# A softplus sum moved from VectorE to TensorE with its string begun sooner, and three in place of two tiles of a shared product made by VectorE

## What is computed

```
x_dbl = xh @ W_x                       # 8 columns dt_low, 16 columns B, 16 columns C
dt = softplus(dt_low @ W_dt + b_dt)    # 256 inner channels
h  = exp(dt * A) * h + dt * B * xh     # 16 states per inner channel, one step per pixel
y  = sum_n(h * C) + xh * D
y  = y * silu(z);  out = y @ W_out
```

## Time and profile before

| | us |
|---|---|
| median of 3 runs | 13842.76 (13840.99 to 13844.69) |
| the profiled execution, its time | 13837.79 |
| its span | 13836.0 |
| DVE busy | 13466.6 (97%) |
| POOL busy | 13246.6 (96%) |
| ACT busy | 12104.2 (87%) |
| PE busy, matmul | 10079.9 (73%), granted clock 0.815 of full |

### The profile page before, as it was taken

The page is one execution under the profiler, slowest core; times in us unless marked ns, Lnnn a source line. Parts: engine busy times, 40 slices in busy tenths (PEclk is TensorE's granted clock), DMA queues, the critical chain, the costliest instruction groups (busy, mean ns, idle before and its releaser), DMA issues.

```text
span 13836.0 us, 170380 instructions
## 1 busy us (share of the span) xinstructions
PE 10079.9 (73%) x34752; PEld 2897.7 (21%) x34752; DVE 13466.6 (97%) x12084; ACT 12104.2 (87%) x24809; POOL 13246.6 (96%) x3076
## 2 busy tenths in 40 slices
PE   6777777777777777777777777777777777777776
PEld 1222222222222222222222222222222222222221
DVE  7999999999999999999999999999999999999999
ACT  7888888888888888888988888888898888888888
POOL 6999999999999999999999999999999999999999
PEclk8888888888888888888878888788888888888887
DMA  6667676666766676666667666666666666666665
GB/s 146 161 154 161 155 163 156 158 157 157 164 156 160 152 163 158 160 157 156 158 159 164 153 163 151 163 159 156 161 153 163 156 161 156 160 156 163 158 155 128
DMA packets 1195180, 2175.99 MB, mean 157 GB/s; under 512 B 152321, under 2 KB 161594, under 8 KB 1194042
## 3 DMA queue, kind: packets, MB, share of 16 engines
q1 hardware_dynamic: 1192762, 2164.07, 66.7%
q10 hardware_dynamic: 1280, 0.02, 0.0%
HBM read 1811.17 MB, written 352.32 MB: 156 GB/s over the span
## 4 chain that ended last, share of the span: by engine, by line
POOL 53%; issue 32%; DVE 6%; ACT 5%; PE 1%; DMA 1%; SPq 0%; POOLq 0%; ACTq 0%; DVEq 0%
POOL hq L1064 38%; POOL dbx L1054 15%; DVE hq L946 4%; ACT ps_a L640 2%; DVE dbx L929 1%; ACT dbx L654 1%; DMA b_rep<-bc_d 0%; DMA dt_d<-dt 0%; DVE pp L905 0%; ACT xh L600 0%; ACT L600 0%; ACT L765 0%; PE ps_acc L456 0%; DMA dtx_d<-sp 0%; POOLq L1063 0%
## 5 line engine op out<-in xcount | busy, mean ns | idle before, releaser
L1064 POOL TENSOR_TENSOR hq<-hq,c_rep 128x2048 f32<-128x2048 f32 x2048 | 9251.0, 4535 | 468.8 <-ACT carry L659 465.0
L946 DVE TENSOR_TENSOR_SCAN hq<-ps_a,dbx 128x512 f32<-128x512 f32 x8192 | 9443.6, 1207 | 128.8 <-ACT dbx L654 47.2
L640 ACT ACTIVATE ps_a<-dt_rep,A_neg 128x512 f32<-128x512 f32 x8192 | 5625.2, 687 | 1294.7 <-DVE hq L946 1231.5
L1054 POOL TENSOR_TENSOR dbx<-dtx_rep,b_rep 128x2048 f32<-128x2048 f32 (+1 forms) x1024 | 4082.1, 3986 | 99.1 <-DMA dtx_rep<-dtx_d 89.1
L654 ACT ACTIVATE dbx<-ps_a,dbx,carry 128x1 f32<-128x1 f32 x7168 | 2504.9, 349 | 240.2 <-POOL dbx L1054 140.4
L929 DVE TENSOR_TENSOR dbx<-dtx_rep,ps_b 128x2048 f32<-128x2048 f32 (+1 forms) x1280 | 2626.7, 2052 | 9.5 <-PE ps_b L444 9.3
L456 PE MATMUL ps_acc<-hq,dsum 128*32 128x512 f32 x16384 | 2334.0, 643 | 292.6 <-POOL hq L1064 292.6
L382 PE MATMUL pp<-sq,w_b1T 128*128 128x512 f32 x512 | 531.1, 1141 | 1608.7 <-ACT sq L579 1608.7
L444 PE MATMUL ps_b<-dbl,bsel 41*128 41x512 f32 x2560 | 1587.3, 703 | 153.3 <-DVE dbx L929 97.7
L400 PE MATMUL pp<-x,W_taps 128*128 128x512 f32 x768 | 693.3, 1002 | 895.2 <-DVE x L900 531.4
L456 PEld LDWEIGHTS ps_acc<-hq,dsum 128*32 128x32 f32 x16384 | 355.9, 111 | 1865.7 <-issue 1046.5
(11 more groups left out here) (123 smaller groups left out, 10466.4 us busy)
## 6 DMA issues: line engine op xcount, KB each, us to landing
dtx_rep<-dtx_d SPq DMA_DIRECT2D x2048, 256.0 KB, 5.4
dt_rep<-dt_d SPq DMA_DIRECT2D x2048, 256.0 KB, 6.3
c_rep<-bc_d SPq DMA_DIRECT2D x1024, 256.0 KB, 4.7
xr<-in_x SPq DMA_DIRECT2D x704, 256.0 KB, 10.9
b_rep<-bc_d SPq DMA_DIRECT2D x2048, 64.0 KB, 5.5
dtx_d<-sp SPq DMA_DIRECT2D x256, 512.0 KB, 2.8
dt_d<-dt SPq DMA_DIRECT2D x256, 512.0 KB, 6.1
xin<-in_x SPq DMA_DIRECT2D x256, 256.0 KB, 10.2
```

The source lines that it names most:

```text
L640: A(ps_a[:, BANK[i], :], dt_rep[:, q // NQ, g, :], ACT.Exp, scale=A_neg[:, q // NQ, q % NQ, g:g + 1]).then_inc(exp_done, 1)
L946: v.tensor_tensor_scan(hq[:, q % HQ, g, :], ps_a[:, BANK[i], :], dbx[:, slot(q), g, :], 0.0, ALU.mult, ALU.add).then_inc(scan_done, 1)
L1054: g.tensor_tensor(dbx[:, slot(q), m:, :], dtx_rep[:, d, m:, :], b_rep[:, q % NQ // 2, :].unsqueeze(1).to_broadcast([P, DG - m, T]), ALU.mu ...
L1064: g.tensor_tensor(quad, quad, c_rep[:, c % 2, q % NQ, :].unsqueeze(1).to_broadcast([P, DG, T]), ALU.mult).then_inc(cmul_done, 1)
```

## The change

VectorE's `softplus` (L905) is removed. W_dt is halved once at the start, so that TensorE leaves v/2 in PSUM. ACT takes |v/2| into `sp` (Abs), exp(-2 |v/2|) into `dt` and ln(1 + that) in place. TensorE adds `sp` and then `dt` onto v/2 in PSUM by matmuls with the identity (`step_sum`, two matmuls of 512 columns each time, in its slots 12 and 14): v/2 + |v/2| = max(v, 0). The last of them raises the semaphore that `dt_x` waits for. On ACT, `evac_dbl` moves from slot 9 to 8, the three steps of the string from 12, 13, 14 to 11, 12, 13, the pooling parts from 10, 11 to 14, 15. The wait for the DMA of the chunk before out of `dt` moves from `evac_dt` to the Exp. On PE, `step_dt` stays in slot 10 but stands ahead of `sum_states` there, and the convolution moves from 11, 12, 13 to 13, 15, 16. `SPLIT` becomes 3: of the shared group DVE makes three tiles, POOL one.

```diff
@@ -53,9 +53,10 @@
 NB = 2
 
 PE_XH, PE_Z, PE_DBL, PE_DT, PE_OUT = (1, 2), (3, 5), 7, 10, 20
-PE_CONV = (11, 12, 13)
+PE_STEP = (12, 14)
+PE_CONV = (13, 15, 16)
 PE_Y, PE_GC, PE_VAR = 19, 24, 27
-ACT_XZ, ACT_DBL, ACT_SP, ACT_DT, ACT_OUT = 5, 9, (12, 13, 14), 17, 23
+ACT_XZ, ACT_DBL, ACT_SP, ACT_DT, ACT_OUT = 5, 8, (11, 12, 13), 17, 23
 ACT_CONV, ACT_GELU, ACT_SQ, ACT_RSTD = 18, 21, 26, 29
 DVE_NORM, DVE_Y1, DVE_DT, DVE_Y0, DVE_GATE = 0, 8, 16, 24, 23
 GN_STATS, GN_SUM, GN_MOM, GN_RSTD, GN_SCALE, GN_SILU = 24, 25, 25, 27, 28, 29
@@ -76,10 +77,10 @@
 assert all(BANK[tile] == BANK[tile - AGE[tile]] for tile in range(NT))
 
 BY_DVE = (0, 2, 3, 4, 6)
-ND, SHARED, SPLIT = len(BY_DVE), 3, 2
+ND, SHARED, SPLIT = len(BY_DVE), 3, 3
 PE_SHARED, DVE_SHARED = 6, 8
 
-POOL_CHUNKS, POOL_SLOTS, ATT_CHUNK = (1, 2, 3, 4), (10, 11), CH - 4
+POOL_CHUNKS, POOL_SLOTS, ATT_CHUNK = (1, 2, 3, 4), (14, 15), CH - 4
 TAP_SPREAD, TAP_MM, TAP_KEEP, TAP_DIAG = 24, 26, 28, (30, 31)
 ATT_FC, ATT_H, ATT_MM, ATT_SUM, ATT_EXP, ATT_WTS = 24, 25, 26, 28, 29, 31
 
@@ -375,6 +376,13 @@
                 if kw == 2:
                     last.then_inc(conv_done, 1)
 
+            def step_sum(b, c, k):
+                pe.wait_ge(sp_done, 3 * (b * CH + c) + (1, 3)[k])
+                for d in range(DI):
+                    last = mm(pp[:, d, :], w["ident"][:], (sp, dt)[k][:, d, :], start=False, stop=True, skip_group_check=True)
+                if k:
+                    last.then_inc(step_done, 1)
+
             def step_y(b, c):
                 pe.wait_ge(y_evac, b * CH + c + 1)
                 if not (isinstance(b, int) and b * CH + c == 0):
@@ -474,6 +482,12 @@
                     for d in range(DI):
                         if u == PE_Z[d]:
                             step_z(b, c, d, alone=c + 1 >= end)
+                    if c + 1 < end:
+                        if u == PE_DT:
+                            step_dt(b, c + 1)
+                        for k in range(2):
+                            if u == PE_STEP[k]:
+                                step_sum(b, c + 1, k)
                     if g == 2:
                         if s >= 2:
                             sum_states(b, c, s - 2)
@@ -484,8 +498,6 @@
                     if c + 1 < end:
                         if u == PE_DBL:
                             step_dbl(b, c + 1)
-                        if u == PE_DT:
-                            step_dt(b, c + 1)
                     if c + 2 < end:
                         for k in range(3):
                             if u == PE_CONV[k]:
@@ -519,6 +531,8 @@
             step_xh(0, 0, 1)
             step_dbl(0, 0)
             step_dt(0, 0)
+            step_sum(0, 0, 0)
+            step_sum(0, 0, 1)
             for kw in (1, 0, 2):
                 step_conv(0, 1, kw)
             step_y(0, 1)
@@ -615,9 +629,11 @@
                 else:
                     act.wait_ge(sp_done, 3 * (b * CH + c) + k)
                     if k == 1:
-                        A(sp[:], sp[:], ACT.Exp, scale=-1.0).then_inc(sp_done, 1)
+                        if not (isinstance(b, int) and b * CH + c == 0):
+                            act.wait_ge(dt_out, 16 * (b * CH + c))
+                        A(dt[:], sp[:], ACT.Exp, scale=-2.0).then_inc(sp_done, 1)
                     else:
-                        A(sp[:], sp[:], ACT.Ln, bias=1.0).then_inc(sp_done, 1)
+                        A(dt[:], dt[:], ACT.Ln, bias=1.0).then_inc(sp_done, 1)
 
             def silu_z(b, c, d):
                 act.wait_ge(z_mm, 2 * (b * CH + c) + d + 1)
@@ -675,8 +691,6 @@
 
             def evac_dt(b, c):
                 act.wait_ge(dtx_done, b * CH + c + 1)
-                if not (isinstance(b, int) and b * CH + c == 0):
-                    act.wait_ge(dt_out, 16 * (b * CH + c))
                 A(dt[:], pp[:, 0:2, :], ACT.Copy).then_inc(dt_done, 1)
 
             def mask_taps(b):
@@ -861,6 +875,7 @@
             v.tensor_scalar(nch_b[:], w["ch_b"][:], -1.0, None, ALU.mult)
             for k in range(2):
                 v.tensor_tensor(W_taps[:, k, :], w["W_in"][:, 0:2 * P], w["cw_rows"][:, k, :], ALU.mult)
+            v.tensor_scalar(w["wdt"][:], w["wdt"][:], 0.5, None, ALU.mult)
             v.memset(x1[:, 0:1], 0.0).then_inc(batch_done, 1)
             dve.wait_ge(batch_done, 1)
 
@@ -899,10 +914,6 @@
                 dve.wait_ge(t2_done, b * CH + c + 1)
                 v.scalar_tensor_tensor(x1_cols(c), pp[:, 2, :], w["vec0"][:, 3:4],
                                        xin[:, c % 2, :], ALU.add, ALU.add).then_inc(x1_done, 1)
-
-            def softplus(b, c):
-                dve.wait_ge(sp_done, 3 * (b * CH + c + 1))
-                v.scalar_tensor_tensor(pp[:, 0:2, :], pp[:, 0:2, :], 0.0, sp[:], ALU.max, ALU.add).then_inc(step_done, 1)
 
             def dt_x(b, c):
                 dve.wait_ge(step_done, b * CH + c + 1)
@@ -990,7 +1001,6 @@
                             norm(b, c + 1)
                             add_input(b, c + 1)
                         if u == DVE_DT:
-                            softplus(b, c + 1)
                             dt_x(b, c + 1)
                     if c + 2 < end:
                         if u == DVE_GATE:
@@ -1015,7 +1025,6 @@
             gate(0, 0)
             norm(0, 0)
             add_input(0, 0)
-            softplus(0, 0)
             dt_x(0, 0)
             gate(0, 1)
             weigh_inputs(0, 0, 0)
```

## The result

The changed kernel takes 13898.92 us (median of 5 runs, 13893.41 to 13930.08) against 13842.46 (13840.96 to 13844.69): ratio 1.0045, 95% interval 1.0034 to 1.0055. It is slower by 0.45%, where 13685 and a range of 13605 to 13785 were forecast. The profiled execution is the slowest of the five (13930.08; span 13928.3), so its sums are read against that.

What follows compares the result with a forecast made beforehand. DVE was taken as the bound, POOL close behind. Softplus -319, third tile +135, dt_x's wait +64, POOL's relief -40 and the start +2 sum to -158 us: 13680 profiled, 13685 as median, range 13605 to 13785.

Steps and rivals of the forecast that it cites:

- rival (d): TensorE makes the second sum at half clock, dt_x waits 2.05 us: slower, +301 us, 14144; chance 0.07.
- DVE is the bound: Over an image DVE works 420.53 of 427.93 us, POOL 413.96, so DVE's work sets the time.
- The new DVE need is 50.65 ... and POOL's is 50.66, so DVE can keep its gain: Inner chunks: DVE falls from 51.37 to 50.65 us and POOL from 51.74 to 50.66, so DVE's saving becomes time.
- -319: Softplus off DVE: 1.25 us saved in each of 255 chunks, -319 us.
- The tile's terms: Third shared tile on DVE: 0.528 us in 256 chunks, +135 us; POOL's relief from it, -40 us.
- The term "-40": POOL's slack removes waits that POOL caused: between 0 and 66 us, taken as -40.
- The Abs then falls into ACT's idle time: On ACT, v/2 stands about 2.3 us before scan 13 ends, so the Abs (1.00 us) fits ahead of tile 15.
- ACT's moves ... 0 net: Exp and Ln only change target and pooling parts go to slots 14 and 15: 0 us net, slots 10 to 13 gain.
- a sign that ACT has become the bound: DVE's busy time falls but the span does not; ACT's waits for scans (1231.5 us) shrink by far more than 100.
- any other lateness of that queue: TensorE's queue late beyond 0.72 us, such as a convolution reaching ACT late: slower, within the half-clock rival's chance of 0.07.
- Rival (a): POOL's relief is worth nothing, taken by the port or ACT's own lateness: -118 us, 13725; chance 0.12.
- The rule that I set beside it: DVE and POOL share an SBUF read port, so work handed from one to the other might not help.

Runs made afterwards that it cites:

- e1: The changed kernel with SPLIT back at 2, so DVE makes two tiles of the shared group and the sum stays on TensorE: 13861.6 us, ratio 1.0016.
- e2: The kernel before with SPLIT 3 alone, softplus staying on DVE: 13903.1 us, ratio 1.0049.
- e3: The changed kernel with ACT copying carry 2 in slot 11 ahead of the Abs, not in slot 12 behind it: 13739.2 us, ratio 0.9934.
- f4: e3 with the first third of the convolution moved on TensorE from slot 13 to 15: 13688.7 us, ratio 0.9891.
- g1: The changed kernel with POOL making the next chunk's input product of group 1 before its product of states 6: 13709.1 us, ratio 0.9903.
- the best version: The changed kernel with carry 2 copied first, convolution later and POOL's input product of group 1 ahead of states 6: 13677.3 us, ratio 0.9878.
- f1: The changed kernel with half of dt_x made twice on DVE in slot 16: 13924.7 us, ratio 1.0064.

## Why the prediction was wrong

**Most prices were right.** Softplus left DVE (-313 us of busy time). The third tile costs 1745 - 1207 = 538 ns (528 said). The shared product on POOL takes 1278 (1284). Added sums: 1.98 us for four records, the second starting at 6265.46 and `dt_x` at 6267.48. The first scan starts 1.6 us later (2 said). The convolution was in time. In the chunk shown the clock stood at full between the sums, and over the run the second sum took more than 2.2 us only once, so rival (d) did not happen there. Two were off: DVE's busy time is 13347, not 13280, and inner chunks last 52.1, not 51.1. `dt_x` waits 73 us (64 said), which is luck: 19 of them are the one wait at the start, and the others fall on 89 chunks, where I had 0.25 in every one.

**The step that failed** is the one that turned these into time: "DVE is the bound", and "The new DVE need is 50.65 ... and POOL's is 50.66, so DVE can keep its gain". I compared the work of two engines over a chunk, and both were under 51. But ACT and POOL form a circle. Its period, 15.88 of ACT's queue and 36.2 of POOL's eight products and the hand-overs, is 52.11, and neither engine's total is in it, nor DVE's. So of -319 nothing arrived: the sum alone came out at +23 us (e1), where its terms gave -253.

The tile's terms erred the other way, and mattered less. It cost 65 us on the kernel before (e2) and 37 on the sum (e1 to the changed kernel), where 135 - 40 = +95 was in the sum. The term "-40" had the right side for the tile: with it DVE's waits for the carry fell both times (47.2 to 35.9, 184.4 to 165.0). That they rose over the whole change, by 118 us, is the work of its other half, the string's new place on ACT.

**"The Abs then falls into ACT's idle time"** was right for tile 15 and wrong for the kernel. I asked what the Abs delays on ACT (tile 15: nothing), not what else stands behind it. That was the copy of carry 2, 0.2 us long, which POOL starts from. In the kernel before POOL already idled 465 us for this copy. Moving it ahead of the Abs gave 160 us, a part of them through the 40 columns.

**"ACT's moves ... 0 net"** overlooked that `evac_dbl` in slot 8 meets TensorE's product of the 40 columns, which is late when the clock is low: 105 us of ACT's waits. The text priced this queue for the second sum alone.

The prediction had named a sign that ACT has become the bound: DVE's busy time falls and the span does not, and ACT's waits for scans shrink from 1231.5 by far more than 100 us. They shrank to 1007.5, by 224. The sign pointed at the right engine.

Rival (d) got the side right by "any other lateness of that queue", at another place; the greater part, the loop, was in no rival. Rival (a), that POOL's relief is worth nothing, was not borne out: 538 ns more on DVE in 256 chunks is 138 us, and the tile cost 65 and 37. Nor did a port show: POOL's 4527 became 4529 ns. The rule that I set beside it, of the Trainium skill's page "Perfetto Trace Analysis", section "Optimizing Scalar/DVE Operations", says that handing over might not help. The trace agrees only in the outcome (the tile did not pay by itself in e2), and its mechanism shows in no row.

What stays open: e3, f4 and g1 cut the loop with three tiles and the sum on TensorE. No run cut it with softplus still on DVE. In the kernel before scan 4 did not wait, so little is to be expected from that, but how much of the 1.2% of the best version needs the sum on TensorE was not measured. Also open is why e3 and f1 have fewer slow products of the 40 columns (30 each, against 61).

## What to carry to other kernels

When engines are near full and wait for each other, write down the circle of waits and add it up once around, the queues of less busy engines included (here ACT, at 87%); compare that with each engine's work. For each piece ask which engine has no idle time in it. Time taken off an engine outside the circle was worth nothing here, and time added beside it counted only beyond the room that was left. Before an instruction is moved in a queue, list the short ones behind it and ask which engine starts from them; a cheap test is the same dummy work in two places.

## What was not expected of the hardware

One and the same product of TensorE took 1.91 or 3.64 us in neighbouring chunks, by the granted clock (1.00 or 0.50 over the product), with the same instructions ahead of it and an idle time of 1.22 or 1.67 us. ACT's wait for it came in the circle, which has no slack, and made the chunk 2.63 us longer. In the changed kernel this product was slow in 61 of 256 chunks.
